# Chunk 2's V projection: first feature half mixed on GpSimd, second in two passes; three of chunk 0's low parts moved to VectorE

## The chip, the cores and the metric

The kernel runs on one core of a Trainium2 chip. The metric is the device time of one launch in microseconds (us), smaller is better. Five queues work beside each other and meet only through semaphores: TensorE (matmuls, PE), VectorE (DVE), ScalarE (ACT), GpSimd (POOL) and SyncE (SP), which here issues DMAs. SBUF is the on-chip memory with 128 partitions; PSUM holds what matmuls write.

## The reference

The input x is 4096 steps of 256 features (float32). One layer of RWKV time mixing, a residual and a layer norm, then a SwiGLU network with 768 hidden features, a residual and a layer norm:

```python
xx = x shifted down by one step (zeros first)
xk = x * mk + xx * (1 - mk)          # the same for v and r, with mv and mr
k, v, r = xk @ Wk.T, xv @ Wv.T, sigmoid(xr @ Wr.T)
y_t = (e^(p-q) aa + e^(u+k-q) v) / (e^(p-q) bb + e^(u+k-q))   # running sums aa, bb, running max p
x = layernorm(x + (r * y) @ Wo.T)
x = layernorm(x + (silu(x @ Wg.T) * (x @ Wu.T)) @ Wd.T)       # Wg, Wu, Wd are int32 / 127
```

A mixed input can be written as `xx + m * (x - xx)`. With `dx = x - xx` this is the last step plus a scaled difference, and its projection is `W xx + W (m * dx)`: the sum of two products. So a projection can be done on the mixed input in one pass, once the mixing has been done, or in two passes, one on the last step (`xt`, straight from memory) and one on the scaled difference.

## The kernel before, in words

Features are on the partitions, in two halves of 128 (h = 0, 1), and time is on the free axis. The 4096 steps are cut into nine chunks (NC = 9): chunks 0 and 8 have 256 steps, the others 512. A round j works on the attention of chunk j, on the feed-forward network of chunk j-1, and prepares the projections of chunk j+1. Each engine has its own written-out program; the order in it is the order of work, and semaphores hold it to the others.

Four PSUM tensors are shared: `bank_a` holds K, the gates and the down-projection, `bank_b` the output projection, the transposed x1 and the up-projection, `bank_c` R, `bank_d` V. An fp32 matmul appears as two records in the trace; the feed-forward matmuls use fp32r, with each input split in a high and a low part (`x1hi`, `x1lo`, `hhi`, `hlo`), and appear as one record each.

**TensorE** (`ffn_products`, L1281, and `round_`, L1310). Round 1: gate and up of chunk 0, six tiles of 128 hidden features (`gate_up`, L1213), the down-projection of chunk 0 (`down`, L1237), the output projection of chunk 1 (`attention_out`, L1182), K of chunk 2, half of R of chunk 2, the transposes of x1, the other half of R. V of chunk 2 is done in two passes, woven into the network of chunk 0: `project_last_step(2, V, [0])` behind tile 3 of gate and up, `[1]` behind tile 5, `project_change(2, 0, V, [0])` behind step 1 of the down-projection and `[1]` behind step 3. Each call is two fp32 products of 512 columns. The last step comes from `xt_of(2)`, which is `xt2`, a view of `y_buf`.

**ScalarE** scales the differences (`scale_dx`, L513), takes the exponentials, SiLU (L591), `hhi` (`hid_high`, L599), `x1` (`norm1`, L526) and `x1hi`. `scale_dx(2, 0, V, 0)` is its last step before round 1, `scale_dx(2, 0, V, 1)` comes behind the second SiLU of round 1.

**GpSimd** (`round_`, L423) computes differences (`diff`, L356), mixings (`mixing`, L366: the scaled difference plus the last step), one sum of the denominator per half (`den_sum`, L372), the low parts of the hidden features (`low_part`, L406: `hlo = hid - hhi`), and the arguments of the output weights (`out_arg`, L380). Before round 1 it computes the differences of chunk 2 (L481 to L483), then reads the flag `wide` into a register and branches on it (L484 to L491). In round 1 it does all six low parts of chunk 0, with the two denominator sums behind the second and the third; then it carries the state, waits until chunk 2's differences are used up (`dx_scaled` and `k2_mixed`), computes those of chunk 3, mixes R of chunk 2, waits for `shift1_ready`, and mixes K and V of chunk 3. In later rounds it does four low parts, and VectorE does the last two.

**VectorE** (`round_`, L929): the scans, the products `hid` (L886), the numerator (L793), the gate (L801), the division `rwkv` (L810), in round 1 also the mixing of K of chunk 2 (`mix_k2`, L1032); then the residuals and statistics, the running maximum of the next chunk, `shift_rows1` (L863), the exponents' arguments and `x1lo`.

`hid` has three slots (NH = 3), so `product(c, m)` waits for the low part of tile m - 3, and the first products of a chunk for the last low parts of the chunk before. `down` waits, step by step, for `hhi` and `hlo`.

Of the kernel before, what the change touches and what calls it, by code (L numbers as in the profile page):

```python
# [14 lines left out]
def rwkv_swiglu_kernel(nc: bass.Bass, xT: bass.AP, x: bass.AP, params: bass.AP, wk: bass.AP, wv: bass.AP,  # L15
                       wr: bass.AP, wo: bass.AP, wg: bass.AP, wu: bass.AP, wd: bass.AP, out: bass.AP):
    f32 = mybir.dt.float32
# [32 lines left out]
    with ctx:  # L50
# [170 lines left out]
        hid_ready = sem("hid_ready")  # L221
        hhi_ready = sem("hhi_ready")
        hlo_ready = sem("hlo_ready")
        hlo_last_ready = sem("hlo_last_ready")
        ffn_ready = sem("ffn_ready")
        res2_ready = sem("res2_ready")
# [43 lines left out]

        def lows_ahead(c):

            return c * NP if first(c) else c * NP + (NM - NP)

        def place(c, i):

# [78 lines left out]
        def _(pool):  # L355
# [67 lines left out]
            def round_(j, s, ffn, ahead):  # L423
                if not last(j) and j > 1:
                    den_sum(j, 0)
                    den_sum(j, 1)
                if ffn:
                    for m in range(NM if j == 1 else NP):
                        low_part(j - 1, m)
                        if j == 1 and m == 1:  # L430
                            den_sum(1, 0)
                        if j == 1 and m == 2:
                            den_sum(1, 1)
                if not last(j):
                    carry_state(j + 1)
                if ahead:
                    if j == 1:
                        pool.wait_ge(dx_scaled, 2 * (3 * CH))
                        pool.wait_ge(k2_mixed, CH)
                        diffs(3)  # L440
                    pool.wait_ge(rwkv_ready, j + 1)
                    if j == 1:
                        mixing(2, 0, R, 0)
                        mixing(2, 0, R, 1, 2 * CH + 1)
                    else:
                        diffs(j + 2)
                    if j == 1:
                        pool.wait_ge(shift1_ready, 2)
                    mix_chunk(j + 2, s, [K, V] if j == 1 else range(3))
                if not last(j):  # L450
                    out_arg(j + 1, 0)
                    out_arg(j + 1, 1)
                    if not last(j + 1):
                        carry_max(j + 2)
                if j == 1:
                    mix_chunk(3, s, [R])
# [24 lines left out]
            for h in range(CH):  # L481
                pool.wait_ge(r1_mixed, h + 1)
                diff(2, h)  # L483
            pool.wait_ge(wide_ready, 1)  # L484
            any_wide = pool.value_load(wide[0:1, 0:1], min_val=0, max_val=1)
            with pool.If(any_wide == 1):
# [236 lines left out]
        def _(dve):  # L723
# [153 lines left out]
            def product(c, m):  # L877
                dve.wait_ge(act_ready, c * NM + (m + 1))
                dve.wait_ge(up_ready, c * NM + (m + 1))

                if m >= NH:
                    dve.wait_ge(hlo_ready, lows_ahead(c) + (m - NH + 1))
                elif c == 1 or (m < NH - (NM - NP) and not first(c)):
                    dve.wait_ge(hlo_ready, lows_ahead(c - 1) + (m + NM - NH + 1))
                n = steps(c)
                nc.vector.tensor_tensor(hid[:, m % NH, 0:n], up_bank(c)[:, m % 2, 0:n], act[:, m % 2, 0:n],  # L886
                                        ALU.mult).then_inc(hid_ready, 1)

            def low_part(c, m):
                dve.wait_ge(hhi_ready, c * NM + (m + 1))  # L890
# [38 lines left out]
            def round_(j, ffn, nxt):  # L929
# [25 lines left out]
                if j == 1:  # L955
                    hidden(5)
                numerator(j)
                if last(j):
                    gate_num(j)
                    hidden(5)  # L960
                    divide(j)
                    low_part(j - 1, NM - 2)
                    low_part(j - 1, NM - 1)
                else:
                    if j != 1:
                        hidden(5)
                    gate_num(j)
                    if j > 1:
                        low_part(j - 1, NM - 2)
                        low_part(j - 1, NM - 1)  # L970
                    divide(j)
                    if j == 1:
                        mix_k2(0)
                        mix_k2(1)
# [137 lines left out]
        def _(pe):  # L1112
# [41 lines left out]
                        if h == CH - 1:  # L1154
                            mm.then_inc(ready, 1)

            def project_last_step(c, i, halves=range(CH)):

                w, bank = ((wkT, bank_a), (wvT, bank_d), (wrT, bank_c))[i]
                pe.wait_ge(xt_in if c == 1 else xt2_in, 16)  # L1160
                if i == K:
                    pe.wait_ge(gap_ready, CH)
                else:
                    pe.wait_ge(num_parts, c)
                for d in halves:
                    for h in range(CH):
                        mm = nc.tensor.matmul(bank[:, d, :], w[:, h, d * P:(d + 1) * P], xt_of(c)[:, h, 0:N],
                                              start=(h == 0), stop=False)
                if c == 1 and i == V and halves[-1] == CH - 1:
                    mm.then_inc(last_steps_done, 1)  # L1170

            def project_change(c, s, i, halves=range(CH)):

                w, bank, ready = ((wkT, bank_a, k_ready), (wvT, bank_d, v_ready), (wrT, bank_c, r_ready))[i]
                for d in halves:
                    for h in range(CH):
                        pe.wait_ge(dx_scaled, (c - 1) * (3 * CH) + place(c, i) * CH + h + 1)
                        mm = nc.tensor.matmul(bank[:, d, :], w[:, h, d * P:(d + 1) * P], mix[:, s, i, h, :],
                                              start=False, stop=(h == CH - 1))
                    mm.then_inc(ready, 1)  # L1180

            def attention_out(c):  # L1182
                pe.wait_ge(rwkv_ready, c + 1)
# [53 lines left out]
            def down(c, tiles, full):  # L1237
                w = wd_f if full else wd_r
                if 0 in tiles:
                    if last(c):  # L1240
                        pe.wait_ge(res2_ready, c * 2)
                    else:
                        pe.wait_ge(act_ready, c * NM + NM)
                for m in tiles:
                    pe.wait_ge(hhi_ready, c * NM + (m + 1))
                    if first(c) or m < NP:
                        pe.wait_ge(hlo_ready, lows_ahead(c) + (m + 1))
                    else:
                        pe.wait_ge(hlo_last_ready, (c - 1) * (NM - NP) + (m - NP + 1))
                    for q in range(steps(c) // P):  # L1250
                        for part in (hhi, hlo):


                            hp = part[:, m, q * P:(q + 1) * P]
                            mm = nc.tensor.matmul(ffn[:, q, :], hp.bitcast(f32) if full else hp, w[:, m, :],  # L1255
                                                  start=(m == 0 and q % 2 == 0 and part is hhi),
                                                  stop=(m == NM - 1 and part is hlo), skip_group_check=True)
                        if m == NM - 1 and q % 2 == 1:
                            mm.then_inc(ffn_ready, halved(c))
# [21 lines left out]
            def ffn_products(j, full):  # L1281
# [5 lines left out]
                    project(1, 1, R)  # L1287
                if isinstance(j, int) and j == 1:
                    gate_up(0, range(2, 4), full)
                    project_last_step(2, V, [0])  # L1290
                    gate_up(0, range(4, NM), full)
                    project_last_step(2, V, [1])
                else:
                    gate_up(j - 1, range(2, NM), full)
                if last(j):
# [3 lines left out]
                elif isinstance(j, int) and j == NC:  # L1299
                    down_last(full)  # L1300
                elif isinstance(j, int) and j == 1:
                    down(0, range(2), full)
                    project_change(2, 0, V, [0])
                    down(0, range(2, 4), full)
                    project_change(2, 0, V, [1])
                    down(0, range(4, NM), full)
                else:
                    down(j - 1, range(NM), full)

            def round_(j, s, ffn, nxt, full=False):  # L1310
                if ffn:
                    ffn_products(j, full)
                if first(j):
                    project_last_step(1, K)
                    project_change(1, 1, K)
                    project_last_step(1, V, [0])
                    pe.wait_ge(wo_in, 16)
                if not last(j):
                    attention_out(j)
                if first(j):  # L1320

                    project_last_step(1, V, [1])
                    project_change(1, 1, V, [0])
                    pe.wait_ge(out_of_range_ready, 1)
                    nc.tensor.matmul(bank_b[0:1, 1, 0:1], ones[:, :], out_of_range[:, :],
                                     start=True, stop=True).then_inc(out_of_range_total, 1)
                    project_change(1, 1, V, [1])
                    pe.wait_ge(ident_ready, 1)
                    pe.wait_ge(wide_ready, 1)
                    return  # L1330
# [72 lines left out]
```

## Time and profile before

| | |
|---|---|
| median of 3 runs | 288.36 us (288.19 to 288.69) |
| the profiled execution | 287.45 us, its span 285.6 us |
| PE busy | 272.8 us (96% of the span) |
| DVE, ACT, POOL busy | 263.6, 213.3, 188.0 us (92, 75, 66%) |
| mean granted TensorE clock | 0.996 |
| round 1 | about 28 to 60 us of the span |

The span is the time from the first to the last instruction in the profile. Start times below count from its beginning. The kernel has a start stretch (to about 26 us) in which loads and the first chunk set the pace, rounds 1 and 2, a long regular stretch, and an end stretch. A busy share is a mean over all of these.

### The profile page before, as it was taken

The numbers are of one execution on the slowest core, as the hardware profiler recorded it, in microseconds if no ns is written. First come the engines' busy times: TensorE is split into PE (matmuls) and PEld (weight loads), VectorE is DVE, ScalarE is ACT, GpSimd is POOL, SyncE is SP. The second block draws the span as 40 slices with busy tenths as digits, with TensorE's granted clock in tenths as the row PEclk, the third lists the DMA queues.
The fourth block names the chain that finished last, engine by engine and source line by source line (L and its number), as shares of the span: only waits on it lengthen the run. The fifth ranks groups of instructions, "written<-read, shape, count | busy, mean of one in ns | idle before, by whom it ended". The sixth has DMA issues, their size and how long they took to land.

```text
span 285.6 us, 4294 instructions
## 1 busy us (share of the span) xinstructions
PE 272.8 (96%) x1258; PEld 198.8 (70%) x1258; DVE 263.6 (92%) x454; ACT 213.3 (75%) x383; POOL 188.0 (66%) x153
## 2 busy tenths in 40 slices
PE   8999999978999999999999999999999999999891
PEld 6654667445875679558874789468965789778791
DVE  5999998999999999999899999999999999888874
ACT  3698874868856986698957986798868982699482
POOL 3738698699978775986688675887476580325051
PEclk9999999999999999999999999999999999999998
DMA  7922200203004001220204020210201020102003
GB/s 236 379 84 75 77 0 0 75 2 110 0 2 147 2 29 47 73 74 0 73 5 147 0 73 0 75 36 0 75 25 50 0 76 0 37 2 75 0 3 115
DMA packets 13573, 16.26 MB, mean 57 GB/s; under 512 B 752, under 2 KB 11248, under 8 KB 13552
## 3 DMA queue, kind: packets, MB, share of 16 engines
q1 hardware_dynamic: 12720, 15.35, 16.5%
q10 hardware_dynamic: 832, 0.66, 0.7%
q8 instruction: 10, 0.16, 0.2%
q14 instruction: 11, 0.09, 0.1%
HBM read 11.81 MB, written 4.19 MB: 56 GB/s over the span
## 4 chain that ended last, share of the span: by engine, by line
PE 63%; ACT 5%; DVE 4%; issue 4%; POOL 2%; DVEq 0%; POOLq 0%; ACTq 0%
PE bank_a L1232 12%; PE bank_b L1232 12%; PE bank_a L1255 11%; PE bank_b L1188 7%; PE bank_c L1139 6%; PE bank_d L1139 6%; PE bank_a L1139 6%; PE bank_b L1209 2%; POOL hlo L411 1%; DVE stats L817 1%; ACT L624 1%; ACT x L533 1%; POOL wts L383 1%; DVE rwkv L810 1%; ACT hhi L604 1%
## 5 line engine op out<-in xcount | busy, mean ns | idle before, releaser
L411 POOL TENSOR_TENSOR hlo<-hid,hhi 128x512 fp32r<-128x512 f32 (+1 forms) x39 | 56.8, 1463 | 33.8 <-ACT hhi L604 33.6
L383 POOL TENSOR_SCALAR wts<-gap,par 128x512 f32<-128x512 f32 (+1 forms) x18 | 35.2, 1956 | 22.3 <-DVE gap L737 21.4
L1255 PE MATMUL bank_a<-wd_r,hhi 128*128 128x256 f32 x180 | 44.7, 290 | 0.1
L1255 PE MATMUL bank_a<-wd_r,hlo 128*128 128x256 f32 x180 | 42.6, 279 | 0.0
L518 ACT ACTIVATE mix<-dx,par 128x512 f32<-128x512 f32 x44 | 28.7, 713 | 17.5 <-POOL dx L363 17.5
L369 POOL TENSOR_TENSOR mix<-mix,xt 128x512 f32<-128x512 f32 (+1 forms) x36 | 39.4, 1131 | 3.0 <-DVE shift L866 2.7
L1255 PEld LDWEIGHTS bank_a<-wd_r,hhi 128*128 128x128 f32 x180 | 33.8, 188 | 2.8 <-issue 2.1
L1232 PE MATMUL bank_a<-x1hi,wg_r 128*128 128x512 f32 (+1 forms) x96 | 32.4, 417 | 3.1 <-ACT x1hi L589 2.3
L510 ACT ACTIVATE wts<-wts 128x512 f32<-128x512 f32 (+1 forms) x54 | 28.1, 580 | 8.9 <-DVE wts L746 8.1
L1255 PEld LDWEIGHTS bank_a<-wd_r,hlo 128*128 128x128 f32 x180 | 33.8, 188 | 0.7 <-issue 0.7
L604 ACT ACTIVATE hhi<-hid 128x512 fp32r<-128x512 f32 (+1 forms) x53 | 30.7, 581 | 4.3 <-DVE hid L886 4.2
L886 DVE TENSOR_TENSOR hid<-bank_b,act 128x512 f32<-128x512 f32 (+1 forms) x48 | 30.8, 643 | 3.1 <-issue 1.1
L596 ACT ACTIVATE act<-bank_a 128x512 f32<-128x512 f32 (+1 forms) x48 | 27.3, 571 | 6.6 <-PE bank_a L1232 6.1
L1232 PE MATMUL bank_b<-x1hi,wu_r 128*128 128x512 f32 (+1 forms) x96 | 29.2, 385 | 0.7 <-DVE hid L886 0.7
L1232 PE MATMUL bank_a<-x1lo,wg_r 128*128 128x512 f32 (+1 forms) x96 | 29.6, 385 | 0.2
L1188 PE MATMUL bank_b<-woT,rwkv 128*128 128x256 f32 x128 | 29.4, 381 | 0.3 <-DVE rwkv L810 0.3
L1232 PE MATMUL bank_b<-x1lo,wu_r 128*128 128x512 f32 (+1 forms) x96 | 28.8, 381 | 0.0
L1139 PE MATMUL bank_c<-mix,wrT 128*128 128x512 f32 (+1 forms) x64 | 27.2, 566 | 0.0
L1188 PEld LDWEIGHTS bank_b<-woT,rwkv 128*128 128x128 f32 x128 | 23.7, 190 | 4.0 <-issue 0.7
L1232 PEld LDWEIGHTS bank_a<-x1hi,wg_r 128*128 128x128 f32 x96 | 17.8, 188 | 11.7 <-issue 6.6
L769 DVE TENSOR_TENSOR_SCAN state<-wts,state,kv 128x512 f32<-128x512 f32 (+1 forms) x18 | 25.7, 1430 | 0.0
L757 DVE TENSOR_TENSOR_SCAN state<-wts,state 128x512 f32<-128x512 f32 (+1 forms) x18 | 25.3, 1404 | 0.0
(130 smaller groups left out, 588.4 us busy)
## 6 DMA issues: line engine op xcount, KB each, us to landing
xrow<-x SPq DMA_DIRECT2D x7, 512.0 KB, 3.7
xt<-xT SPq DMA_DIRECT2D x6, 513.0 KB, 3.6
out<-y_buf SPq DMA_DIRECT2D x6, 512.0 KB, 2.9
wg_i<-wg SPq DMA_DIRECT2D x1, 768.0 KB, 7.9
wu_i<-wu SPq DMA_DIRECT2D x1, 768.0 KB, 9.3
wd_i<-wd SPq DMA_DIRECT2D x1, 768.0 KB, 11.1
out<-y_buf SPq DMA_DIRECT2D x3, 256.0 KB, 2.3
y_buf<-xT SPq DMA_DIRECT2D x1, 513.0 KB, 10.1
```

The costliest lines, as they stand in the source:

```text
L369: nc.gpsimd.tensor_tensor(mix[:, s, i, h, 0:n], mix[:, s, i, h, 0:n], xt_of(c)[:, h, 0:n], ALU.add).then_inc(mixed, count)
L383: nc.gpsimd.tensor_scalar(wts[:, OUT, h, 0:n], gap[:, h, 0:n], par[:, FIRST, h:h + 1], CAP, ALU.add, ALU.min).then_inc(out_arg_ready, 1)
L411: nc.gpsimd.tensor_tensor(hlo[:, m, 0:n], hid[:, m % NH, 0:n], hhi[:, m, 0:n].bitcast(f32), ALU.subtract).then_inc(hlo_ready, 1)
L510: nc.scalar.activation(wts[:, i, h, 0:n], wts[:, i, h, 0:n], ACT.Exp, scale=-1.0 if i == IN_OLD else 1.0).then_inc(wts_ready, 1)
L518: nc.scalar.activation(mix[:, s, i, h, 0:n], dx[:, h, 0:n], ACT.Copy, scale=par[:, MIX + i, h:h + 1]).then_inc(dx_scaled, count)
L596: nc.scalar.activation(act[:, m % 2, 0:n], gate_bank(c)[:, m % 2, 0:n], ACT.Silu, scale=SCALE).then_inc(act_ready, 1)
L604: nc.scalar.activation(hhi[:, m, 0:n], hid[:, m % NH, 0:n], ACT.Copy).then_inc(hhi_ready, 1)
L886: nc.vector.tensor_tensor(hid[:, m % NH, 0:n], up_bank(c)[:, m % 2, 0:n], act[:, m % 2, 0:n], ALU.mult).then_inc(hid_ready, 1)
L1139: mm = nc.tensor.matmul(bank[:, d, 0:n], w[:, h, d * P:(d + 1) * P], mix[:, s, i, h, 0:n], start=(h == 0), stop=(h == CH - 1))
L1188: mm = nc.tensor.matmul(attn[:, 2 * q if last(c) else q, :], rwkv[:, h, q * P:(q + 1) * P], woT[:, h, :], start=(h == 0), stop=(h == CH - 1))
L1232: mm = nc.tensor.matmul(bank[:, m % 2, 0:steps(c)], w[:, h, m * P:(m + 1) * P], xp, start=(h == 0 and part is x1hi), stop=(h == CH - 1 and ...
L1255: mm = nc.tensor.matmul(ffn[:, q, :], hp.bitcast(f32) if full else hp, w[:, m, :], start=(m == 0 and q % 2 == 0 and part is hhi), stop=(m ...
```

## The change

V of chunk 2 is split by input feature. The first 128 features (h = 0) are mixed on GpSimd, right behind the differences of chunk 2, and projected in one pass; the second 128 keep their two passes. TensorE has six fp32 products for V of chunk 2 instead of eight, in three stretches instead of four. The low parts 3, 4 and 5 of chunk 0 move from GpSimd to VectorE: number 3 between the numerator and the gate of chunk 1, numbers 4 and 5 between the gate and the division. They count on a semaphore of their own, `hlo0_ready`. GpSimd does three low parts in round 1 instead of six. The counts of `mixed` and of `hlo_ready` are fitted: R's second mixing of chunk 2 adds CH + 2 instead of 2 * CH + 1.

```diff
         def lows_ahead(c):
-            return c * NP if first(c) else c * NP + (NM - NP)
+            return c * NP if first(c) else c * NP + (NH - NP)
...
 # GpSimd, round_
-                    for m in range(NM if j == 1 else NP):
+                    for m in range(NH if j == 1 else NP):
                         low_part(j - 1, m)
...
-                        mixing(2, 0, R, 1, 2 * CH + 1)
+                        mixing(2, 0, R, 1, CH + 2)
...
 # GpSimd, before round 1
             for h in range(CH):
                 pool.wait_ge(r1_mixed, h + 1)
                 diff(2, h)
+            mixing(2, 0, V, 0)
             pool.wait_ge(wide_ready, 1)
             any_wide = pool.value_load(wide[0:1, 0:1], min_val=0, max_val=1)
...
 # VectorE, product
-                elif c == 1 or (m < NH - (NM - NP) and not first(c)):
+                elif c == 1:
+                    dve.wait_ge(hlo0_ready, m + 1)
+                elif m < NH - (NM - NP) and not first(c):
...
+            def low_part_first(m):
+                dve.wait_ge(hhi_ready, m + 1)
+                n = steps(0)
+                nc.vector.tensor_tensor(hlo[:, m, 0:n], hid[:, m % NH, 0:n], hhi[:, m, 0:n].bitcast(f32),
+                                        ALU.subtract).then_inc(hlo0_ready, 1)
...
 # VectorE, round_
                 numerator(j)
+                if j == 1:
+                    low_part_first(NH)
...
                     gate_num(j)
+                    if j == 1:
+                        low_part_first(NH + 1)
+                        low_part_first(NH + 2)
...
 # TensorE
+            def v2_mixed():
+
+                pe.wait_ge(mixed, 1)
+                pe.wait_ge(num_parts, 2)
+                for d in range(CH):
+                    nc.tensor.matmul(bank_d[:, d, :], wvT[:, 0, d * P:(d + 1) * P], mix[:, 0, V, 0, :],
+                                     start=True, stop=False)
+
+            def v2_last_step():
+
+                pe.wait_ge(xt2_in, 16)
+                for d in range(CH):
+                    nc.tensor.matmul(bank_d[:, d, :], wvT[:, 1, d * P:(d + 1) * P], xt_of(2)[:, 1, 0:N],
+                                     start=False, stop=False)
+
+            def v2_change():
+                pe.wait_ge(dx_scaled, 3 * CH + place(2, V) * CH + 2)
+                for d in range(CH):
+                    nc.tensor.matmul(bank_d[:, d, :], wvT[:, 1, d * P:(d + 1) * P], mix[:, 0, V, 1, :],
+                                     start=False, stop=True).then_inc(v_ready, 1)
...
 # down
-                    if first(c) or m < NP:
+                    if first(c) and m >= NH:
+                        pe.wait_ge(hlo0_ready, m - NH + 1)
+                    elif first(c) or m < NP:
...
 # ffn_products, round 1
                     gate_up(0, range(2, 4), full)
-                    project_last_step(2, V, [0])
+                    v2_mixed()
                     gate_up(0, range(4, NM), full)
-                    project_last_step(2, V, [1])
+                    v2_last_step()
...
                     down(0, range(2), full)
-                    project_change(2, 0, V, [0])
-                    down(0, range(2, 4), full)
-                    project_change(2, 0, V, [1])
-                    down(0, range(4, NM), full)
+                    v2_change()
+                    down(0, range(2, NM), full)
```

## Rows read from the trace of the kernel before

**Rows 1.** Busy time by stretches: us, then each engine's busy us and instructions, clock, DMA.

```profile
47.50:60.00 12.50, 11.62 (x42) 6.67 (x40) 11.43 (x24) 7.91 (x16) 9.68 (x9) 1.00 0.16 43
...
75.00:232.00 157.00, 156.88 (x715) 114.20 (x715) 151.97 (x250) 125.19 (x214) 114.99 (x90) 1.00 0.14 43
```

**Rows 2.** The chain that ended last: start us, us, what.

```profile
61.53 2.01 POOL wts L383
...
84.54 3.43 PE bank_a L1139 x8
```

**Rows 3.** Timeline of TensorE: start us, us, engine, line, operation, count [idle before <-releaser].

```profile
35.94 1.96 PE L1167 MATMUL bank_d<-y_buf,wvT 128*128 128x512 f32 x4
...
44.88 1.88 PE L1178 MATMUL bank_d<-mix,wvT 128*128 128x512 f32 x4
...
47.54 3.62 PE L1188 MATMUL bank_b<-woT,rwkv 128*128 128x256 f32 x16
...
60.87 0.89 PE L1232 MATMUL bank_a<-x1hi,wg_r 128*128 128x512 f32 x2 [1.45 <-ACT x1hi L589]
```

**Rows 4.** Timeline of GpSimd, 29 to 60 us.

```profile
29.01 3.33 POOL L363 TENSOR_TENSOR dx<-y_buf 128x512 f32<-128x512 f32 x2
34.87 1.44 POOL L411 TENSOR_TENSOR hlo<-hid,hhi 128x256 fp32r<-128x256 f32 x2 [2.52 <-ACT hhi L604]
...
41.07 5.05 POOL L411 TENSOR_TENSOR hlo<-hid,hhi 128x256 fp32r<-128x256 f32 x3
...
47.47 2.03 POOL L363 TENSOR_TENSOR dx<-xt 128x512 f32<-128x512 f32 x2 [0.75 <-issue]
...
54.52 4.78 POOL L369 TENSOR_TENSOR mix<-mix,xt 128x512 f32<-128x512 f32 x4 [2.72 <-DVE shift L866]
```

**Rows 5.** Timeline of VectorE, 26 to 60 us.

```profile
27.46 0.76 DVE L874 TENSOR_TENSOR x1lo<-bank_b,x1hi 128x256 fp32r<-128x256 f32 x2
...
29.45 2.06 DVE L757 TENSOR_TENSOR_SCAN state<-wts,state 128x512 f32<-128x512 f32 x1
...
32.01 1.41 DVE L757 TENSOR_TENSOR_SCAN state<-wts,state 128x512 f32<-128x512 f32 x1
...
36.05 1.33 DVE L769 TENSOR_TENSOR_SCAN state<-wts,state,kv 128x512 f32<-128x512 f32 x1
...
40.35 1.84 DVE L793 TENSOR_TENSOR num<-num,state 128x1024 f32<-128x1024 f32 x1
42.23 1.64 DVE L801 SCALAR_TENSOR_TENSOR num<-recv,num 128x1024 f32<-128x1024 f32 x1
43.98 1.57 DVE L810 TENSOR_TENSOR rwkv<-num,den 128x1024 f32<-128x1024 f32 x1
...
47.82 0.69 DVE L919 SCALAR_TENSOR_TENSOR res<-bank_a,x 128x512 f32<-128x512 f32 x1 [0.48 <-PE bank_a L1255]
...
53.13 1.25 DVE L730 TENSOR_TENSOR_SCAN pmax<-neg_decay,pmax,bank_a 128x512 f32<-128x512 f32 x1
54.30 0.14 DVE L866 SCALAR_TENSOR_TENSOR shift<-mv,rstd 128x4 f32<-128x4 f32 x1
```

**Rows 6.** What VectorE waited for, 18 to 75 us: us in total, times, longest.

```profile
DVE res L830 <- PE bank_b L1188: 0.4, 2, 0.2
```

**Rows 7.** Mixing, line 369, inputs of chunk 2: ns minimum, median, maximum; first and last start.

```profile
L369 POOL TENSOR_TENSOR mix<-mix,y_buf x2: 1092/1187/1282, 49.5 to 50.7; 128x512 f32<-128x512 f32 x2
```

**Rows 8.** Timeline of ScalarE, 26 to 60 us.

```profile
30.46 0.72 ACT L518 ACTIVATE mix<-dx,par 128x512 f32<-128x512 f32 x1 [0.68 <-POOL dx L363]
...
49.54 3.18 ACT L518 ACTIVATE mix<-dx,par 128x512 f32<-128x512 f32 x5 [0.27 <-POOL dx L363]
53.12 0.30 ACT L572 ACTIVATE lnv<-mv,eps 128x4 f32<-128x4 f32 x1 [0.40 <-DVE mv L822]
```

**Rows 9.** VectorE's groups, 70 to 240 us: busy us, mean ns | idle before.

```profile
L810 DVE TENSOR_TENSOR rwkv<-num,den 128x1024 f32<-128x1024 f32 x6 | 7.3, 1223 | 1.6 <-ACT den L558 1.6
```

**Rows 10.** K mixing of chunk 2, line 1035: ns minimum, median, maximum.

```profile
L1035 DVE SCALAR_TENSOR_TENSOR mix<-dx,par,y_buf x2: 740/974/1209, 45.5 to 46.6; 128x512 f32<-128x512 f32 x2
```

More of the change, by code:

```diff
@@ L223, in rwkv_swiglu_kernel @@
         hlo_ready = sem("hlo_ready")
+        hlo0_ready = sem("hlo0_ready")
         hlo_last_ready = sem("hlo_last_ready")
@@ L1155, in project_first, with project_last_step @@
                             mm.then_inc(ready, 1)
-            def project_last_step(c, i, halves=range(CH)):
+            def project_last_step(i, halves=range(CH)):
                 w, bank = ((wkT, bank_a), (wvT, bank_d), (wrT, bank_c))[i]
-                pe.wait_ge(xt_in if c == 1 else xt2_in, 16)
+                pe.wait_ge(xt_in, 16)
                 if i == K:
@@ L1163, in project_last_step, with project_change @@
                 else:
-                    pe.wait_ge(num_parts, c)
+                    pe.wait_ge(num_parts, 1)
                 for d in halves:
                     for h in range(CH):
-                        mm = nc.tensor.matmul(bank[:, d, :], w[:, h, d * P:(d + 1) * P], xt_of(c)[:, h, 0:N],
+                        mm = nc.tensor.matmul(bank[:, d, :], w[:, h, d * P:(d + 1) * P], xt[:, h, 0:N],
                                               start=(h == 0), stop=False)
-                if c == 1 and i == V and halves[-1] == CH - 1:
+                if i == V and halves[-1] == CH - 1:
                     mm.then_inc(last_steps_done, 1)
-            def project_change(c, s, i, halves=range(CH)):
+            def project_change(i, halves=range(CH)):
                 w, bank, ready = ((wkT, bank_a, k_ready), (wvT, bank_d, v_ready), (wrT, bank_c, r_ready))[i]
@@ L1176, in project_change @@
                     for h in range(CH):
-                        pe.wait_ge(dx_scaled, (c - 1) * (3 * CH) + place(c, i) * CH + h + 1)
-                        mm = nc.tensor.matmul(bank[:, d, :], w[:, h, d * P:(d + 1) * P], mix[:, s, i, h, :],
+                        pe.wait_ge(dx_scaled, i * CH + h + 1)
+                        mm = nc.tensor.matmul(bank[:, d, :], w[:, h, d * P:(d + 1) * P], mix[:, 1, i, h, :],
                                               start=False, stop=(h == CH - 1))
                     mm.then_inc(ready, 1)
+            def v2_mixed():
[14 more added lines that the diff above has]
+                                     start=False, stop=True).then_inc(v_ready, 1)
             def attention_out(c):
@@ L1313, in round_ @@
                 if first(j):
-                    project_last_step(1, K)
-                    project_change(1, 1, K)
-                    project_last_step(1, V, [0])
+                    project_last_step(K)
+                    project_change(K)
+                    project_last_step(V, [0])
                     pe.wait_ge(wo_in, 16)
@@ L1320, in round_ @@
                 if first(j):
-                    project_last_step(1, V, [1])
-                    project_change(1, 1, V, [0])
+                    project_last_step(V, [1])
+                    project_change(V, [0])
                     pe.wait_ge(out_of_range_ready, 1)
@@ L1326, in round_ @@
                                      start=True, stop=True).then_inc(out_of_range_total, 1)
-                    project_change(1, 1, V, [1])
+                    project_change(V, [1])
                     pe.wait_ge(ident_ready, 1)
```

## The prediction

> **What bounds the kernel now.** I read the busy time by stretches first. From 75 to 232 us TensorE is busy 156.88 of 157.00 us, so there the end moves only with TensorE's own work or with the moment at which the stretch begins; from 47.5 to 60 us it is busy 11.62 of 12.50, and something else sets the pace [rows 1]. The chain that ended last begins, so far as it can be followed back, with GpSimd's `wts<-gap` at 61.53 and goes over ScalarE to the first SiLU of the next round [rows 2]. That GpSimd operation stands behind four mixings of 4.78 us in all, begun at 54.52, which had waited 2.72 us for VectorE's `shift` [rows 4], an operation of 0.14 us at 54.30 [rows 5]. ScalarE's row normalisation waits for the same `shift`, and behind it TensorE waits 1.45 us for `x1hi` at 60.87 [rows 3]. So the question is: how much earlier does `shift` of chunk 1 run? What lies behind it, to 75 us, hangs on it through operations of the same lengths, and the full stretch then carries the difference to the end.
>
> Back from `shift`: it stands behind the scan `pmax` at 53.13. From the sum `res` at 47.82 to that scan VectorE worked without a stop but for two waits on the output projection, 0.35 us together (0.20 and 0.15 in the timeline, 0.4 as grouped), and it had waited 0.48 us for the down-projection before 47.82 [rows 5, 6]. The output projection began at 47.54 [rows 3], when the down-projection of chunk 0 was through; `rwkv`, its other input, was there at 43.98 + 1.57 = 45.55 [rows 5]. So TensorE's queue sets that start now, with 2.0 us to spare behind it on VectorE's side.
>
> **The change, part by part.**
>
> (a) TensorE. V of chunk 2 is now four stretches of four records, 1.88 to 1.96 us each, begun at 35.94, 39.57, 42.23 and 44.88; the first and the last stand in [rows 3]. They are eight fp32 products of two records each. The change has six products: two on the mixed first half, two on the last step, two on the change. One stretch goes. Eight such records take 3.43 us on the chain where nothing stands between them [rows 2], 0.43 each, so 4 x 0.43 = 1.72 us go. The remaining three start where the first three start now; what follows is the four remaining steps of the down-projection in one piece. It would end at about 47.43 - 1.72 = 45.7, and the output projection could start at 45.8.
>
> (b) GpSimd, added before round 1: one mixing of 128x512. The same operation on the same inputs took 1.09 and 1.28 us [rows 7]. Its input is there at 30.46 + 0.72 = 31.2 [rows 8], the queue is free when the two differences end, at 32.34, and the next operation, the low part 0, began at 34.87 after 2.52 us of idleness [rows 4]. So 1.1 to 1.3 us lie inside a gap of 2.5. VectorE's scan of 32.01 is already running; the rows show that where both engines read two SBUF operands one stands until the other is done (the scan at 29.45 took 2.06 beside the differences, the one at 36.05 took 1.33 [rows 5]). So the mixing stands until the scan ends at about 33.4, runs to about 34.45, and costs VectorE nothing: by the code what follows there until 36.05 reads one operand from PSUM. What the trace does not show is the flag that GpSimd reads into a register, with a branch, between the mixing and low part 0. Bounds: 0, if it overlaps the mixing, and 34.87 - 32.34 = 2.5 us, if it fills the whole gap now and starts only behind the mixing. It may use up to 34.87 - 34.45 = 0.4 us for free. I take 0.1 us of delay: the gap as it stands ends at the landing of `hhi` (ScalarE releases it [rows 4]), so nothing shows that the flag needs it.
>
> (c) GpSimd, removed: three low parts, 5.05 us from 41.07, which two uncontended ones at 34.87 would make in 1.44 [rows 4]. The difference is waiting in turns with VectorE.
>
> (d) VectorE, added: three low parts of 128x256. Nearest row: two such subtractions in 0.76 us [rows 5], 0.38 each, 0.35 from start to start: about 1.05 us. Bounds 1.0 to 1.25.
>
> (e) VectorE, given back: the numerator took 1.84 us, the gate 1.64, the division 1.57 [rows 5], against a mean of 1.22 for a 128x1024 product in the quiet stretch [rows 9]. The numerator's excess is GpSimd's `den`, which stays. The gate gets back 0.4, the division 0.35, and the first of the two K mixings 1.21 - 0.74 = 0.47 [rows 10]: 1.2 us. So: numerator to 42.2, low part 3 to 42.5, gate to 43.65, low parts 4 and 5 to 44.3, division to 45.45 (ScalarE's reciprocal, 43.9, is no longer last), K mixings to 46.85 instead of 47.35. The low parts are in time: TensorE asks for number 5 at about 45.2. `rwkv` at 45.45 is just before the 45.8 at which TensorE is ready for it; VectorE's slack of 2.0 us has shrunk to 0.3.
>
> (f) What is late next. The sum `res` at 47.82 follows the K mixings at once at 46.85: 0.50 us of earlier end and 0.48 of idleness gone. The two waits on the output projection go as well, 0.35: its halves land 1.7 us earlier, VectorE asks only 1.0 to 1.3 earlier, and it had missed them by 0.2. `pmax` at 53.13 - 1.33 = 51.80, `shift` at 52.97. On ScalarE the six scalings of chunk 3 end at 52.72 now (49.54 + 3.18) and hang on GpSimd's differences at 47.47 [rows 4, 8], which wait for the K mixings: they end at 52.2, the logarithm takes 0.30 [rows 8] and the root about as much, so `rstd` is there at 52.8, just before 52.97. GpSimd's two R mixings end at about 51.3, TensorE's first half of K at about 51.1, both in time.
>
> The sum: 1.33 us, less 0.1 for (b): 1.25. TensorE's 1.72 is the ceiling; 0.4 of it is kept back by VectorE. The other edits (semaphore, counts, thresholds) only rename waits; `product` of chunk 1 waits for low parts that are long done, and the loads of `xt` wait for the same totals of `mixed`. The profiled execution took 287.45 (span 285.60): it would become 286.2. The median shown is 288.36, 0.91 above it; the same difference gives 287.1.
>
> **A rule weighed.** In [rows 5] the gate beside a low part took 0.42 more than in the quiet stretch, the scan at 29.45 0.73 more than at 36.05. The Trainium skill, Advanced Engine Details and Errata, VectorE Performance Modes, says that GpSimd and VectorE's two-port modes block each other, and names no others; SBUF — State Buffer, two separate sides, adds to these VectorE operations with two SBUF inputs. By the first alone part (e) would give nothing back (rival 3); by the second the sum stands as above. The rows go with the second. The first page also says, under Sequencer and Instruction Queues, that engine instructions can be queued while a control instruction executes; no run here shows it for the flag. By it the delay in (b) would be nothing.
>
> **Rivals.**
>
> 1. The flag comes late, by a middling amount. If low part 0 slips by up to 0.45 us, low part 1 still starts before the scan of 36.05 and pushes it by as much: the gain falls to 0.9. If it slips more, low part 1 stands behind that scan, the first `den` behind the next, and low part 2, product 5 and the numerator come 1.0 us later: the gain is 0.35. Middle 0.65: 287.7. For it: no row shows the flag's time; against it: nothing waits for the flag now.
>
> 2. The other side. The flag fills the gap now (2.4 us) and cannot start before the mixing has ended. Then low part 0 is free at 36.9 and stands behind the scan to 37.4; product 3 slips to 38.1, the numerator ends at 43.9, 1.7 late, the K mixings at 48.55. `pmax` follows 4.95 later (51.80 - 46.85), at 53.5, and `shift` at 54.7: 0.4 later than now, 288.8. It decides from a flag of about 2 us. Against it: it would need the flag to end just when `hhi` lands.
>
> 3. VectorE gets nothing back. Then the three low parts are 1.05 us of pure cost: the K mixings end at 48.4, `pmax` starts at 53.35 and `shift` 0.2 later than now: 288.6. Against it: three rows with excess.
>
> 4. VectorE hides nothing of the 1.72: 286.65. It would need another 0.4 us from it, say by less standing beside `den`.
>
> **How the numbers follow.** My case, gain 1.0 to 1.5: 0.56. Rival 1: 0.18, half of it above 0.58 us. Rival 2: 0.06. Rival 3: 0.08. Rival 4: 0.04. The rest, 0.08, are effects on timing in the long stretch of either sign. The three runs shown differ by 0.5 us, so 0.2% (0.58 us) is about what can be told from no change. Faster by more than that: 0.56 + 0.09 + 0.04 + 0.01 = 0.70. Slower: 0.03 of rival 2, 0.02 of 3, 0.05 of the rest = 0.10. Within: 0.20. The range runs from rival 4 (286.6) to just beyond rival 3 (288.7); rival 2 is left out. My case by itself is 286.8 to 287.4.
>
> **What would show it.** Right: three stretches on V of chunk 2, the last begun near 42.2; the mixing ending near 34.5 with VectorE's scan of 36.05 in its place; low part 0 within 0.2 of 34.87; gate near 1.2 us; division ended near 45.5; output projection at 45.8; `pmax` at 51.8; `shift` at 53.0; everything from 75 us on earlier by the same 1.25. Wrong: low part 0 later than 35.3 (rivals 1 and 2); gate and division still above 1.5 us (rival 3); `shift` early, but the first SiLU of round 2 not.

## The result, and the profile after

The changed kernel took 286.90 us (median of 6, 286.31 to 287.17) against 288.27 us for the kernel before (median of 6, 288.04 to 288.69): 1.37 us less, ratio 0.9950, 95% interval 0.9939 to 0.9960. Two later series gave ratios of 0.9939 (0.9925 to 0.9953) and 0.9951 (0.9939 to 0.9964). The forecast was 287.1.

The timeline of TensorE in the changed kernel: start us, us, engine, line, operation, count, and in brackets the idle time before it and what ended it.

```profile
35.96 1.96 PE L1202 MATMUL bank_d<-mix,wvT 128*128 128x512 f32 x4
...
42.24 1.88 PE L1215 MATMUL bank_d<-mix,wvT 128*128 128x512 f32 x4
...
45.84 3.61 PE L1224 MATMUL bank_b<-woT,rwkv 128*128 128x256 f32 x16
...
59.37 0.90 PE L1268 MATMUL bank_a<-x1hi,wg_r 128*128 128x512 f32 x2 [1.47 <-ACT x1hi L591]
```

Chunk 2's V has three stretches, on the mixed half (35.96), on the last step (39.58, not copied) and on the change (42.24). The fourth is gone, and the output projection starts at 45.84 instead of 47.54 [rows 3]. The wait ahead of `x1hi` is about as long as before, 1.47 us for 1.45, but ends 1.50 us earlier.

GpSimd:

```profile
32.32 2.19 POOL L370 TENSOR_TENSOR mix<-mix,y_buf 128x512 f32<-128x512 f32 x1
34.88 1.45 POOL L412 TENSOR_TENSOR hlo<-hid,hhi 128x256 fp32r<-128x256 f32 x2 [0.37 <-ACT hhi L606]
...
42.28 0.32 POOL L398 COPY state<-state 128x4 f32<-128x4 f32 x1 [1.15 <-DVE num L795]
46.95 2.03 POOL L364 TENSOR_TENSOR dx<-xt 128x512 f32<-128x512 f32 x2 [4.35 <-issue]
...
53.01 4.78 POOL L370 TENSOR_TENSOR mix<-mix,xt 128x512 f32<-128x512 f32 x4 [1.74 <-DVE shift L868]
```

The added mixing is the line at 32.32. It ends at 34.51. VectorE's scan in front of it ends at 33.44 (32.03 + 1.41), so of the 2.19 us it stands for 1.12 and works for 1.07. Low part 0 starts at 34.88, where it started at 34.87 [rows 4], and still waits 0.37 us for `hhi`: the flag between the two costs nothing here. After the state's copy at 42.28 GpSimd now idles until the differences of chunk 3.

VectorE:

```profile
42.13 0.41 DVE L896 TENSOR_TENSOR hlo<-hid,hhi 128x256 fp32r<-128x256 f32 x1
42.47 1.21 DVE L803 SCALAR_TENSOR_TENSOR num<-recv,num 128x1024 f32<-128x1024 f32 x1
43.61 0.75 DVE L896 TENSOR_TENSOR hlo<-hid,hhi 128x256 fp32r<-128x256 f32 x2
44.28 1.21 DVE L812 TENSOR_TENSOR rwkv<-num,den 128x1024 f32<-128x1024 f32 x1
45.41 1.40 DVE L1050 SCALAR_TENSOR_TENSOR mix<-dx,par,y_buf 128x512 f32<-128x512 f32 x2
46.74 0.68 DVE L929 SCALAR_TENSOR_TENSOR res<-bank_a,x 128x512 f32<-128x512 f32 x1
...
51.63 1.25 DVE L732 TENSOR_TENSOR_SCAN pmax<-neg_decay,pmax,bank_a 128x512 f32<-128x512 f32 x1
52.79 0.14 DVE L868 SCALAR_TENSOR_TENSOR shift<-mv,rstd 128x4 f32<-128x4 f32 x1
```

The lines at 42.13 and 43.61 are the three low parts, 0.41 and 0.75 us. Between them the gate takes 1.21 us instead of 1.64, behind them the division 1.21 instead of 1.57 and the two K mixings 1.40 instead of 1.87 [rows 5, 10]. `res` follows at 46.74 without a wait. `pmax` comes at 51.63 instead of 53.13, `shift` at 52.79 instead of 54.30.

ScalarE, the scalings of chunk 3 and the logarithm behind them:

```profile
49.02 3.17 ACT L520 ACTIVATE mix<-dx,par 128x512 f32<-128x512 f32 x5 [0.28 <-POOL dx L364]
52.10 0.28 ACT L574 ACTIVATE lnv<-mv,eps 128x4 f32<-128x4 f32 x1
```

The scalings end at 52.19; the logarithm that starts at 52.10 has lost its idle time [rows 8]. The row root `rstd` ends at 52.61, 0.18 us before `shift` starts: ScalarE is nearly level with VectorE here.

The chain that ended last, start us and us:

```profile
83.03 3.43 PE bank_a L1154 x8
```

This is K of chunk 3, at 84.54 before [rows 2]: 1.51 us earlier. The issue of the last stores, on the DMA queue, in the kernel before and then in the changed one:

```profile
281.59 1.06 SPq L317 DMA_DIRECT2D out<-mix  x2
```

```profile
280.26 1.05 SPq L318 DMA_DIRECT2D out<-mix  x2
```

1.33 us earlier. From K of chunk 3 to this issue it was 197.05 us before and 197.23 after. In the ten other profiles it was 197.0 to 197.2 (197.06 and 197.07 in the two more of the changed kernel), so 0.2 us is scatter, and otherwise the gain is carried through. The span is only 0.5 us shorter (285.6 and 285.1). The rest is the landing: from this issue to the end of the span it was 4.0 us in the first profile, 4.8 in the second, and 4.15 to 4.8 in ten more, without regard to the kernel. That is why the medians, not the two profiled times (287.45 and 287.01), give the size.

### The profile page after: what moved, and what is told of

It is laid out like the page before. It is cut to its first block, busy times and chain, and to the rows that moved or that the text cites. A ratio compares the mean times of both kernels' runs of the same rounds, so it can differ in the third digit from the quotient of the medians.

```text
span 285.1 us, 4284 instructions
## 1 busy us (share of the span) xinstructions
PE 272.3 (96%) x1254; PEld 199.9 (70%) x1254; DVE 263.2 (92%) x457; ACT 212.6 (75%) x383; POOL 184.8 (65%) x151
## 4 chain that ended last, share of the span: by engine, by line
PE 79%; DVE 10%; ACT 4%; issue 4%; POOL 1%; DVEq 0%; POOLq 0%; ACTq 0%
PE bank_b L1268 14%; PE bank_a L1268 14%; PE bank_a L1293 12%; PE bank_b L1224 8%; PE bank_c L1154 6%; PE bank_d L1154 6%; PE bank_a L1154 6%; PE bank_b L1245 2%; DVE stats L819 2%; PE bank_c L1132 1%; POOL hlo L412 1%; PE bank_d L1193 1%; PE bank_d L1182 1%; PE bank_a L1193 1%; PE bank_a L1182 1%
## 5 line engine op out<-in xcount | busy, mean ns | idle before, releaser
L412 POOL TENSOR_TENSOR hlo<-hid,hhi 128x512 fp32r<-128x512 f32 (+1 forms) x36 | 51.8, 1445 | 32.0 <-ACT hhi L606 31.9
L364 POOL TENSOR_TENSOR dx<-xt 128x512 f32<-128x512 f32 (+1 forms) x14 | 13.4, 980 | 19.3 <-DVE rwkv L812 14.9
```

The lines of the kernel that those rows point to most:

```text
L412: nc.gpsimd.tensor_tensor(hlo[:, m, 0:n], hid[:, m % NH, 0:n], hhi[:, m, 0:n].bitcast(f32), ALU.subtract).then_inc(hlo_ready, 1)
```

## The experiments

The start stretch, in which the loads arrive, moves everything behind it by up to 1.0 us from one profile to the next. So times below are also given from T, the start of VectorE's first state scan of chunk 1 (29.45 in the kernel before, 29.47 in the changed one). "K3" is the start of K of chunk 3 on the chain that ended last, the last point before TensorE alone sets the pace.

| kernel | ratio to before (95%) | output projection - T | pmax - T | shift to second pmax scan | K3 - pmax | K3 - T |
|---|---|---|---|---|---|---|
| before | 1 | 18.09 | 23.68 | 0.33 | 31.41 | 55.09 |
| changed | 0.9950 (0.9939 to 0.9960) | 16.37 | 22.16 | 0.14 | 31.40 | 53.56 |
| the same, second series | 0.9939 (0.9925 to 0.9953) | 16.37 | 22.15 | 0.13 | 31.39 | 53.54 |
| the same, third series | 0.9951 (0.9939 to 0.9964) | 16.39 | 22.16 | 0.15 | 31.33 | 53.49 |
| V alone | 0.9974 (0.9963 to 0.9985) | 17.35 | 22.95 | 0.33 | 31.38 | 54.33 |
| low parts alone | 0.9998 (0.9989 to 1.0007) | 18.09 | 23.68 | 0.33 | 31.34 | 55.02 |
| spare subtractions | 1.0025 (1.0010 to 1.0039) | 17.67 | 23.76 | 0.06 | 31.86 | 55.62 |
| spare mixing | 1.0015 (1.0000 to 1.0029) | 16.91 | 22.99 | 0.06 | 32.83 | 55.82 |
| late V | 0.9984 (0.9971 to 0.9998) | 16.07 | 22.15 | 0.05 | 31.85 | 54.00 |
| late V and a memset | 0.9949 (0.9935 to 0.9963) | 16.07 | 22.15 | 0.19 | 31.40 | 53.55 |
| arguments early | 0.9959 (0.9946 to 0.9972) | 16.37 | 22.17 | 0.13 | 31.64 | 53.81 |
| arguments between | 0.9948 (0.9934 to 0.9962) | 16.38 | 22.16 | 0.15 | 31.47 | 53.63 |

**V alone.** The low parts stay on GpSimd.

```diff
-                    for m in range(NH if j == 1 else NP):
+                    for m in range(NM if j == 1 else NP):
```

The low parts on VectorE, and their waits, are taken out as well.

> The changed kernel with all six low parts of chunk 0 back on GpSimd: V's new order alone. My theory (TensorE's queue is 1.72 us shorter, but the last low part lands at 46.1 as before and VectorE is not relieved): output projection at 46.65, K mixings end at 47.35 as before, pmax at 52.25, shift at 53.4; gain 0.9 us, 287.4. Rival A, the low parts' move adds nothing: 286.9, as the full change. Rival B, the shorter queue is worth nothing without the move: 288.3.

```profile
46.51 0.35 PE L1284 MATMUL bank_a<-wd_r,hhi 128*128 128x256 f32 x1 [0.76 <-POOL hlo L412]
...
47.04 3.62 PE L1217 MATMUL bank_b<-woT,rwkv 128*128 128x256 f32 x16
```

TensorE waits 0.76 us for the last low part of GpSimd, and the output projection starts 0.74 earlier than before instead of 1.72. VectorE, not relieved, is what is late:

```profile
45.70 1.87 DVE L1043 SCALAR_TENSOR_TENSOR mix<-dx,par,y_buf 128x512 f32<-128x512 f32 x2
47.49 0.68 DVE L927 SCALAR_TENSOR_TENSOR res<-bank_a,x 128x512 f32<-128x512 f32 x1
```

Its K mixings take 1.87 us as before, and `res` follows them at once. `pmax` gains 0.73; the ratio says 0.75 (0.0026 x 288.07). I had 0.9; from T, both the output projection and `pmax` came 0.15 us later than I had them. Rival A (the gain of the full change) and rival B (none) lie outside the interval.

**Low parts alone.** V in eight products, the three low parts on VectorE.

> The kernel before with the low parts 3 to 5 of chunk 0 on VectorE, V as before in eight products. My theory: VectorE's K mixings end at 46.75 instead of 47.35, but it then waits 1 us for the down-projection; output projection at 47.5, pmax at 53.1, no gain: 288.3. Rival A, VectorE's relief is half of the gain by itself: 287.8. Rival B, the three subtractions cost VectorE more than it gets back: slower, 288.6.

```profile
45.72 1.40 DVE L1049 SCALAR_TENSOR_TENSOR mix<-dx,par,y_buf 128x512 f32<-128x512 f32 x2
48.14 0.69 DVE L928 SCALAR_TENSOR_TENSOR res<-bank_a,x 128x512 f32<-128x512 f32 x1 [1.02 <-PE bank_a L1271]
```

VectorE's K mixings end early, and it waits 1.02 us for the down-projection instead of 0.48 [rows 5]. Nothing is gained, as expected; rival A (0.5 us faster) and rival B (0.3 slower) lie outside the interval. So the two parts bring 0.73 and 0 alone and 1.5 together at `pmax`: each takes away the wait that hides the other.

**Spare subtractions.** In the changed kernel GpSimd does three more subtractions into an unused buffer. VectorE's products of chunk 1 also wait until they are done.

```diff
                             den_sum(1, 1)
+                            for k in range(NH, NM):
+                                pool.wait_ge(hhi_ready, k + 1)
+                                nc.gpsimd.tensor_tensor(spare[:, k - NH, :], hid[:, k % NH, 0:N // 2],
+                                                        hhi[:, k, 0:N // 2].bitcast(f32), ALU.subtract)
...
                     dve.wait_ge(hlo0_ready, m + 1)
+                    dve.wait_ge(state_carried, 2)
```

> The changed kernel with three more subtractions on GpSimd, of the same inputs into a buffer that nobody reads, where the low parts 3 to 5 stood. My theory, the two engines take turns when both read two SBUF operands: gate, division and first K mixing grow by 0.4 to 0.5 us each, K mixings end near 47.95, pmax at 52.8: 1.2 us slower than the changed kernel, 288.1 (287.9 to 288.4). Rival, no turns (the excess seen before had another cause): no change, 286.9.

GpSimd, then VectorE:

```profile
40.66 4.25 POOL L438 TENSOR_TENSOR spare<-hid,hhi 128x256 f32<-128x256 f32 x3
```

```profile
41.70 0.95 DVE L902 TENSOR_TENSOR hlo<-hid,hhi 128x256 fp32r<-128x256 f32 x1
42.58 1.75 DVE L808 SCALAR_TENSOR_TENSOR num<-recv,num 128x1024 f32<-128x1024 f32 x1
44.25 1.28 DVE L902 TENSOR_TENSOR hlo<-hid,hhi 128x256 fp32r<-128x256 f32 x2
```

VectorE computed nothing more, and the added wait held nothing up (the state was carried at 45.25, the first of those products came at 67.19, behind a wait for SiLU). But low part 3 took 0.95 instead of 0.41, the gate 1.75 instead of 1.21, low parts 4 and 5 1.28 instead of 0.75: about 0.54 us for each operation that GpSimd adds, 1.60 at `pmax`. I had the turns right, but not which operations take them, nor the sum of 1.2. This is the exclusive pair of the Trainium skill, SBUF — State Buffer, two separate sides; the note in the Trainium skill, Advanced Engine Details and Errata, VectorE Performance Modes, which names only VectorE's two-port modes, does not cover it: by that note alone the three would have stayed at 0.41, 1.21 and 0.75. The total is 2.1 to 2.5 us above the changed kernel (ratios 1.0025 against 0.9939 to 0.9951), where I had 1.2. Beyond the 1.60, 0.46 is in the column "K3 - pmax", on which more below.

**Spare mixing.** One more addition on GpSimd between V's mixing and the flag.

```diff
             mixing(2, 0, V, 0)
+            nc.gpsimd.tensor_tensor(spare[:, :], dx[:, 0, :], xt2[:, 0, 0:N], ALU.add)
```

> The changed kernel with a second addition of 128x512 on GpSimd, into a buffer that nobody reads, between V's mixing and the flag. My theory (my rival 1, that a late low part 0 is passed on with interest): low part 0 begins at 35.6 plus what of the flag is exposed (0 to 0.4), low part 1 stands behind VectorE's scan, the numerator ends 1.2 us later than in the changed kernel: 288.1. Rival, the slip is absorbed: 286.9 to 287.1. Rival, passed on one to one: 287.6.

GpSimd, then VectorE:

```profile
34.49 1.30 POOL L487 TENSOR_TENSOR spare<-dx,y_buf 128x512 f32<-128x512 f32 x1
35.76 2.33 POOL L413 TENSOR_TENSOR hlo<-hid,hhi 128x256 fp32r<-128x256 f32 x2
38.05 2.01 POOL L379 TENSOR_TENSOR den<-wts,state 128x512 f32<-128x512 f32 x1
```

```profile
36.09 1.48 DVE L773 TENSOR_TENSOR_SCAN state<-wts,state,kv 128x512 f32<-128x512 f32 x1
...
40.88 0.42 DVE L892 TENSOR_TENSOR hid<-bank_b,act 128x256 f32<-128x256 f32 x1 [1.39 <-POOL hlo L413]
```

Low part 0 starts at 35.76, 0.03 us before the spare addition's record ends: with 1.3 us of work in front of it the flag is still not seen, so it overlaps the work ahead and rival 2 of the prediction is ruled out. The slip of 0.86 us (from T) is passed on as 0.83 at `pmax`: product 5 waits 1.39 us for low part 2 instead of 0.34, but the second scan stands less (1.36 us instead of 1.73). So up to `pmax` "passed on one to one" was right, my 1.2 was not.

The whole kernel missed all three, though: ratio 1.0015 against 0.9939 to 0.9951, 1.8 to 2.2 us above the changed kernel. Behind `pmax` the profile has 1.43 us more than the changed kernel's; both parts of it come up below, 0.45 with late V and 1.0 with the clock.

**Late V.** V's last pass of chunk 2 behind R, in TensorE's idle time.

```diff
                     down(0, range(2), full)
-                    v2_change()
                     down(0, range(2, NM), full)
...
                     project(j + 1, s, R, [1] if isinstance(j, int) and j == 1 else range(CH))
+                    if isinstance(j, int) and j == 1:
+                        v2_change()
```

> The changed kernel with V's last pass of chunk 2 (1.72 us on TensorE) taken out of the down-projection and put behind R, into TensorE's idle 1.47 us ahead of x1hi. My theory, VectorE sets the pace from the division on: output projection at 45.5 instead of 45.84, pmax still at 51.6, the pass fills the gap and makes the first gate matmul 0 to 0.2 late: 286.9 to 287.1. Rival, TensorE's queue is still what bounds: pmax earlier by 0.3 or more, 286.6 or less.

The output projection starts 0.30 us earlier and `pmax` not at all (22.15): in the changed kernel VectorE sets the pace there. But the kernel came out slower than the changed one, by 1.0 to 1.3 us by the ratios, and in the profile 0.45 us longer behind `pmax`, which no theory had. VectorE, GpSimd and TensorE:

```profile
53.09 0.14 DVE L868 SCALAR_TENSOR_TENSOR shift<-mv,rstd 128x4 f32<-128x4 f32 x1
53.14 1.28 DVE L732 TENSOR_TENSOR_SCAN pmax<-neg_decay,pmax,bank_a 128x512 f32<-128x512 f32 x1
...
57.33 1.04 DVE L936 SCALAR_TENSOR_TENSOR shift<-mv,rstd 128x2 f32<-128x2 f32 x1
```

```profile
58.45 5.26 POOL L384 TENSOR_SCALAR wts<-gap,par 128x512 f32<-128x512 f32 x2
```

```profile
66.33 0.73 PE L1268 MATMUL bank_a<-x1hi,wg_r 128*128 128x512 f32 x2 [2.18 <-ACT act L598]
```

The same two places in the changed kernel:

```profile
57.99 0.15 DVE L936 SCALAR_TENSOR_TENSOR shift<-mv,rstd 128x2 f32<-128x2 f32 x1
```

```profile
57.88 4.13 POOL L384 TENSOR_SCALAR wts<-gap,par 128x512 f32<-128x512 f32 x2
```

The small `shift` of 128x2 at 57.33 takes 1.04 us, and GpSimd's two `out_arg` 5.26 us, against 0.15 and 4.13 in the changed kernel; `x1hi` is ready early, the first SiLU late, and TensorE waits 2.18 us for it. In the table the three kernels with this pattern are those in which the second scan follows `shift` by 0.05 or 0.06 us. That suggested the next one.

**Late V and a memset.** Late V with a write of 128x128 zeros on VectorE between the two, nothing else.

```diff
                 shift_rows1(j)
+                if j == 1:
+                    nc.vector.memset(spare[:, :], 0.0)
                 running_max(j + 1, 1)
```

> V's last pass late, with a memset of 128x128 on VectorE in round 1 between shift and the second pmax scan: about 0.15 us more work, nothing else. In the traces so far the second scan starts 0.13 to 0.33 us behind shift in the kernels where K of chunk 3 follows pmax by 31.4 us, and 0.05 us behind it in those where it follows by 31.85. Theory, which engine gets the next turn at the shared SBUF operands is decided by such a shift: with the memset the second scan starts 0.2 later, K of chunk 3 follows pmax by 31.4 again and the kernel is 0.4 us faster than without it, 287.0. Rival, the 0.45 us come from the late V pass itself: 31.85 or more, 287.5.

```profile
53.01 0.14 DVE L869 SCALAR_TENSOR_TENSOR shift<-mv,rstd 128x4 f32<-128x4 f32 x1
53.12 0.17 DVE L1034 MEMSET spare<- 128x128 f32 x1
53.20 1.16 DVE L733 TENSOR_TENSOR_SCAN pmax<-neg_decay,pmax,bank_a 128x512 f32<-128x512 f32 x1
...
58.21 0.15 DVE L937 SCALAR_TENSOR_TENSOR shift<-mv,rstd 128x2 f32<-128x2 f32 x1
```

```profile
58.10 4.14 POOL L385 TENSOR_SCALAR wts<-gap,par 128x512 f32<-128x512 f32 x2
```

The second scan started 0.14 us later against `shift`, GpSimd's pair took 4.14 us again, and K3 came 0.45 us earlier from T than without the memset: more work, and faster. So the late pass alone does not make the long stretch. That the offset of the second scan does, by deciding who gets the turns, fits all twelve profiles (0.05 and 0.06 with 31.85 or more, 0.13 and above with 31.64 or less) but is argued: the memset is also a write of its own, and no run moves the scan in another way. The ratios (0.9949 against 0.9984, intervals just apart, in two series) say 1.0 us, and the two profiles 0.45. A part of the rest goes with the granted clock, averaged over each execution. Of late V's twelve, the five at 0.995 and above have a median of 287.16 us and the seven at 0.992 and below one of 287.96; of the memset's six only one is at 0.992 or below. The spare mixing has 287.40 and 287.76 at 0.998 and a median of 288.57 in the other ten, at 0.992 and below. In each of the changed kernel's three series, executions below 0.994 differ from the others by less than 0.3 us. This kernel is level with the changed one.

**Arguments early, arguments between.** In the changed kernel GpSimd's two `out_arg` of chunk 2 go ahead of both V mixings of chunk 3, or of the last.

```diff
-                    mix_chunk(j + 2, s, [K, V] if j == 1 else range(3))
+                    mix_chunk(j + 2, s, [K] if j == 1 else range(3))
...
-                    mix_chunk(3, s, [R])
+                    mix_chunk(3, s, [V, R])
```

> The changed kernel with GpSimd's two out_arg of chunk 2 (round 1) ahead of the V mixings of chunk 3 instead of behind them; V's two go in front of R's. Theory, the chain from shift to the first SiLU of round 2 runs through GpSimd: out_arg ends 2 us earlier, ScalarE's last exponential about 0.7 us earlier, TensorE's 0.76 us wait for SiLU goes: 0.7 to 1.0 us faster than the changed kernel, 285.7. Rival, ScalarE and VectorE are as late as GpSimd there: no more than 0.2 us.

> As args_early, with only the last V mixing of chunk 3 behind the two out_arg. Theory: ScalarE's exponentials behind x1hi are then the limit in both, so the same gain of 0.7 us, 285.7 to 286.0. Rival, GpSimd still bounds: half of the other's gain, 286.3.

The first SiLU of round 2 came 9.20 us behind `shift` instead of 11.20 (10.28 in the second kernel), as meant. The gain was then given back. What VectorE waited for from 60 to 80 us, in the early kernel and in the changed one:

```profile
DVE hid L890 <- POOL hlo L412: 2.3, 2, 1.8
```

```profile
DVE hid L890 <- POOL hlo L412: 0.2, 1, 0.2
```

The mixings pushed behind the arguments delay the low parts of chunk 1, and VectorE waits 2.3 us for them instead of 0.2. GpSimd has no idle time to speak of from its first mixing behind `shift` to the state's copy, and in the early kernel the same work took it longer:

```profile
55.84 4.59 POOL L384 TENSOR_SCALAR wts<-gap,par 128x512 f32<-128x512 f32 x2
...
60.64 6.47 POOL L370 TENSOR_TENSOR mix<-mix,xt 128x512 f32<-128x512 f32 x4
```

With 2.32 us for the first two mixings that is 13.4 us, against 12.2 in the changed kernel (4.78, 4.13 and 3.26). Part of that is won back in the low parts, and the state's copy starts 46.35 us behind T instead of 46.1. In the same series the changed kernel took 286.73 us, the early one 286.86, the one between 286.52, with overlapping intervals. So both theories, 0.7 us or more, failed. The rival of the first, no more than 0.2 us, has the number right but not the reason, since the SiLU did come 2 us earlier; the half gain that the second's rival gave was not seen clear of noise. No version here beats the changed kernel by more than the noise.

**The changed kernel again**, beside the others.

> The changed kernel itself beside the others. 286.9 by the runs so far. The profiled time ended 1.34 us earlier at the last arithmetic but only 0.5 us at the last store; if the last store's landing is noise, the next profile shows the last VectorE operation again near 280.5 and another distance to the end of the span.

> The changed kernel beside these three, for a comparison on one chip: ratio to before 0.994 to 0.995, K of chunk 3 begins 53.55 us behind the first scan of chunk 1's state.

K3 - T is the same within 0.07 us in its three profiles. The distance from the last issue of stores to the end was 4.8, 4.6 and 4.15 us, so the landing varies with the run.

## Why the prediction was right

The mechanism stood at every step that the prediction named; the size at `shift` was 1.51 us where it said 1.33 less 0.1 (1.23, which it rounded to 1.25). The medians differ by 1.22 to 1.80 us in the three series, so that the first, 1.37, comes within 0.12 of the forecast is in part luck. The 286.2 us given for a profiled execution was 287.01, because of the landing.

- (a) The 1.72 us on TensorE: output projection at 45.84 for 45.8. Right.
- (b) Mixing ended at 34.51 for 34.45, and VectorE's scan behind it started at 36.07 for 36.05, no later from T: no cost. The 0.1 us of delay for the flag was not there, and the spare mixing shows that the flag hides behind what is queued ahead of it.
- (c), (d) Low parts on VectorE: start to start they took 0.34 us (42.13 to 42.47) and 0.67 for two, 1.01 for the three against 1.05.
- (e) Given back: 0.43 at the gate, 0.36 at the division, 0.47 at the K mixings; 1.26 for 1.2. The spare subtractions put it back and cost 1.60, so the turns are the cause of what VectorE gained.
- (f) `res` at 46.74 for 46.85 and `pmax` at 51.63 for 51.80. The term that was off is the 4.95 us between the two: 4.89 measured from start to start, and `res` started 0.07 before the record of the K mixings ended, which I had counted to its end. ScalarE's root was in time, as said.
- VectorE held back part of the 1.72: 22.16 against 23.68 is 1.52, so 0.2 us, not 0.4. Late V shows the same from the other side: there TensorE is ready 0.30 us earlier still, and `pmax` does not move.
- Rivals 1 and 2 needed a late flag; low part 0 moved by 0.01 us. Rival 3 is refuted by the gate's 1.21. Rival 4 (a gain of 1.72, chance 0.04) was nearer than that let it seem: the 1.52 us at `pmax` lie midway between it and the sum's 1.33, and at the upper edge of the 1.0 to 1.5 called "my case". That each part alone would bring 0.9 and 0, and not the whole, was expected by the same reasoning before those two ran, and held in kind (0.73 and 0).

What I had not seen is that the stretch behind `shift` need not keep its length. I took "operations of the same lengths" for granted; it held here (31.40 for 31.41) but was off by 0.45 us or more in three of the other kernels, and by 0.2 with the arguments early.

## What to carry to other kernels

When two engines arrive at one point nearly level, try relieving both in the same change: here V alone brought 0.73 us, the low parts alone 0, both 1.5. Cost a moved operation on GpSimd or VectorE by what the other is reading at that moment: three subtractions of 0.72 us cost VectorE 1.6 us where it reads two SBUF operands, and a mixing of 1.1 us nothing where it reads PSUM. Before calling a few tenths explained, compare how long the unchanged stretch behind takes, and at what granted clock each execution ran.

## What the runs showed of the hardware

The granted clock of TensorE fell for some microseconds in three of the twelve profiles: the changed kernel's first, V alone (0.66 from 60 to 65 us) and the spare mixing. The lines are from the changed kernel and from the spare mixing (us, then busy us and instructions by engine, granted clock, DMA):

```profile
60.00:65.00 5.00, 4.91 (x14) 3.68 (x14) 5.00 (x5) 4.56 (x7) 4.92 (x4) 0.66 0.01 3
```

```profile
68.00:69.00 1.00, 1.00 (x3) 0.75 (x3) 1.00 (x2) 1.00 (x3) 1.00 (x1) 0.50 0.87 228
```

The last idle time of TensorE before the first, up to 59.37, was 1.47 us, before the second, up to 66.88, 2.19. The first, at 0.50 from 62 to 64 us (1.2 of 2.4 GHz), fell into a stretch where TensorE would else have waited for SiLU, and K3 - T is 53.56 with it and 53.49 and 53.54 without. The second fell where TensorE was on the path, and K3 - pmax is 32.83, against 31.85 and 31.86 in the two kernels with the same pattern and full clock: 1.0 us. The changed kernel's second profile had the same wait as its first, late V and the spare subtractions one of 2.18 us, all three at full clock, so what brings the fall is left open.

In the three kernels where TensorE waits 2.2 us for SiLU, the executions with the lower mean clock took 0.6 to 1.0 us longer than the others, by the medians; in the other kernels the difference was at most 0.4. Where the clock fell in the executions without a profile is not on record. And a kernel with a 0.17 us memset more was faster, its pair of `out_arg` back from 5.26 to 4.14 us: where VectorE and GpSimd take turns, tenths of a microsecond can matter.
